# Two chained cross-attention and feed-forward layers: the maxima of block 0 and block 8 copied from ScalarE's queue, loads moved later, and the last feed-forward chunk in halves

## The chip, the cores and the metric
The kernel runs on one core of a Trainium2 chip. The metric is device time in microseconds (us). Engines: TensorE (PE, its weight loads PEld), VectorE (DVE), ScalarE (ACT), GpSimd (POOL), SyncE (SP, which here only issues DMAs). ScalarE issues DMAs as well, on a queue of its own. SBUF is the on-chip memory with 128 partitions, PSUM holds the eight accumulator banks of 128 x 512 f32.

## The reference
`x` is 4 x 1024 x 256, the context 4 x 77 x 256, all f32.
```
x = x + xattn0(layernorm(x), ctx, mask)   # 16 heads of 16, biases, softmax over 77 keys
x = x + experts(layernorm(x))             # 6 experts, the best 2 by a router, gelu
x = x + xattn1(layernorm(x), ctx)         # 16 query heads, one shared key and value head
x = x + ffn(layernorm(x))                 # 256 -> 1024 -> 256
  h = round256(h1 + b1);  y = piecewise-linear gelu(h) on 32 segments, round256
  out = round256(y @ w2 + b2)             # round256: to multiples of 1/256
```
Products are made to f32 accuracy: each operand is split into a high part (fp32r) and a low rest, and three products are added.

## The kernel before
The 4096 rows of x are eight blocks (G) of 512. Every engine has one program written out by hand in `build`; they meet only by semaphores (`wait_ge`, `then_inc`). There is no planner: what stands ahead in an engine's code runs first.

**Setup and the attention of block 0.** Keys, values and the first block's queries are made. A score of head i is one product of a stacked operand: `qst` holds per head pair, on partitions 0 to 95, high and low parts of the queries (`stack_queries`, L249, three DMAs of 256 KB for each half c of the heads, SBUF to SBUF), on partitions 96 and 97 the negated row maxima (`stack_maxima`, L260, one DMA of 32 KB in 16 rows of 2 KB) and on 98 to 127 part of the mask (`stack_low`, L242: 47 rows of 2 KB into `mm`, then 240 rows of 2 KB into `qst`). `l_kst` is the stacked key operand (twelve DMAs, L912). The maxima come from `max_unit` (PE), `take_maxima` (DVE), `turn_maxima` (PE) and `maxima` (ACT, writes `mt`). The first score of a block (`score`, i = 0, L400) waits for `mt_stacked`, `low_moved`, `stacked[0]`, and so for these DMAs; i = 8 waits for `stacked[1]`. `leading(G, c)` (ACT, L298) may overwrite `qh` only when the stacking DMAs of the block before have landed.

SP's code (L896 on) issues in this order for block 0: `stack_low`, six key copies, queries c = 0, six key copies, the maxima, queries c = 1, then mask 1 and two loads of 1 MB of x (L921). In the loop over G it then issues for block n = G + 1: `stack_low`, the queries of both halves, the mask of n + 1, the maxima of n. DMAs of one issuing engine go through one queue. In the loop, while block G is scored, block n's queries and maxima are made, the one after is normed, and block p = G - 1 is divided and projected.

**Values.** `vall` needs four batches b of two products of context and Wv and one of the bias (L1522); PE makes them after the maxima of block 0 were turned. ACT norms block 1 (L1138) and then copies the values (L1140).

**POOL in the setup** norms block 1 (`invert(1)`), then builds the masked keys of batches 1 to 3 (L1004, 16 operations), `wol`, then the mask parts of block 1.

**Layer 1** starts after the experts, as block G = 8 (`BLOCKS`): SP issues queries c = 0, the maxima, queries c = 1 (L959), and then the row loads `row0` (512 KB, the first row of w1 broadcast) and `rows` (L963). From G = 9 on the loop of L966 is used.

**The feed-forward** runs k = 0 to 63, eight chunks of 128 features for each block. Each chunk passes `hidden` (PE), `early` (DVE, writes `ffixed`), `gelus` (ACT, two), `climb` (POOL, `frise`), `interpolate` (DVE, `fpart`), `grow` (POOL) or `finish` (DVE, `fy`), `leading` (ACT, two: rounding in bank `YR`, then `fyh`), `rest` (DVE, `fyl`) and `output` (PE, 12 products). `YR` is one bank, so the leading of k waits for the rest of k - 1 (L744). At the end come `round_output` (ACT), `add` (DVE, two halves) and one store of 512 KB per block (L976).

## Time and profile before
| | |
|---|---|
| median of 3 runs | 789.33 us (789.02 to 789.87) |
| the profiled execution | 787.69 us, its span 785.5 us |
| busy share of the span | PE 93%, PEld 70%, DVE 82%, ACT 65%, POOL 47% |
| chain that ended last | PE 54%, DVE 19%, issue 8%, ACT 7%, DMA 7%, POOL 4% |
| DMA in the chain | qst<-mt 5% |
| mean granted TensorE clock | 0.991 of full |

The span runs from the first to the last instruction on the core; 2.2 us of the execution lie outside. "Issue" in the chain is time in which an engine waited for nothing that the profile attributes, so a wait for a DMA whose landing it could not pair may stand there. Times in the rows are us from the span's start.

### The profile page before, as it was taken

The page shows a single profiled execution, that of the slowest core. Times are in us where ns is not written, and L with a number is a line of the kernel's source. Part 1 is how long each engine was busy: PE and PEld are TensorE (multiplying, and loading weights), DVE is VectorE, ACT ScalarE, POOL GpSimd, SP SyncE. Part 2 cuts the span into 40 slices and gives each one's busy share as a digit, 9 for nine tenths or more (in the row PEclk, how much of TensorE's full clock was granted, in tenths as well). Part 3 has the DMA queues.
Part 4 walks back from the last instruction along what each step waited for, and adds up shares of the span by engine and source line. Part 5 has one row for each costly group of instructions (what it writes and reads, how often), then busy time and mean ns, then how long its engine had stood idle before and what let it go on. Part 6 is the DMA issues. An engine that isn't in the chain of part 4 may idle for free.

```text
span 785.5 us, 13554 instructions
## 1 busy us (share of the span) xinstructions
PE 729.2 (93%) x4372; PEld 549.3 (70%) x4372; DVE 644.6 (82%) x1546; ACT 514.0 (65%) x943; POOL 373.0 (47%) x323
## 2 busy tenths in 40 slices
PE   4799999999999999999997999999989999999995
PEld 3566666766558888888874555555568888888985
DVE  7648778777878878888897888998788999999995
ACT  3446556565654456555436777677778989989885
POOL 6374444334222223232214232232259999999884
PEclk9889999999999999999999999999999999999999
DMA  7975634654210000001029665755200000000001
GB/s 234 134 209 121 139 76 93 119 120 88 68 36 1 1 1 7 1 1 55 1 41 143 89 82 76 131 76 77 30 1 1 2 28 28 28 28 2 28 28 54
DMA packets 25101, 48.64 MB, mean 62 GB/s; under 512 B 3686, under 2 KB 7016, under 8 KB 24520
## 3 DMA queue, kind: packets, MB, share of 16 engines
q1 hardware_dynamic: 23366, 46.54, 30.6%
q10 hardware_dynamic: 1666, 1.24, 0.5%
q8 instruction: 36, 0.59, 0.3%
q14 instruction: 33, 0.27, 0.1%
HBM read 12.12 MB, written 4.19 MB: 21 GB/s over the span
## 4 chain that ended last, share of the span: by engine, by line
PE 54%; DVE 19%; issue 8%; ACT 7%; DMA 7%; POOL 4%; SPq 0%; ACTq 0%; DVEq 0%; POOLq 0%
PE bank L141 15%; PE bank L649 6%; PE bank L436 6%; PE bank L413 6%; DMA qst<-mt 5%; PE bank L424 5%; PE bank L388 5%; DVE mx L342 4%; PE bank L416 3%; DVE fpart L768 3%; PE bank L812 3%; PE bank L391 2%; DVE x L617 2%; DVE fyl L780 2%; DVE ffixed L762 2%
## 5 line engine op out<-in xcount | busy, mean ns | idle before, releaser
L316 ACT ACTIVATE pt<-bank 77x512 f32<-77x512 f32 x256 | 141.1, 589 | 78.2 <-PE bank L416 58.3
L342 DVE TENSOR_REDUCE mx<-bank 128x4 f32<-128x308 f32 x256 | 109.0, 471 | 22.5 <-PE bank L391 12.3
L413 PE MATMUL bank<-qst,l_kst 128*77 128x512 f32 (+1 forms) x256 | 102.8, 417 | 15.8 <-DMA qst<-mt 9.8
L721 POOL TENSOR_TENSOR frise<-fg,fg 128x512 f32<-128x512 f32 x64 | 101.3, 1583 | 6.7 <-ACT fg L739 1.5
L388 PE MATMUL bank<-l_kblk,qh 128*128 128x308 f32 x256 | 81.3, 336 | 10.1 <-DVE mx L342 5.7
L284 POOL TENSOR_TENSOR ol<-ot,oh 128x512 fp32r<-128x512 f32 x32 | 41.4, 1294 | 94.4 <-ACT oh L321 50.2
L617 DVE SCALAR_TENSOR_TENSOR x<-bank,eweight,x 128x256 f32<-128x256 f32 x192 | 79.6, 477 | 4.1 <-PE bank L649 3.8
L413 PEld LDWEIGHTS bank<-qst,l_kst 128*77 128x77 f32 (+1 forms) x256 | 36.5, 146 | 65.1 <-ACT pt L316 24.1
L103 POOL TENSOR_TENSOR rstd<-var,minus_half 128x4 f32<-128x4 f32 x32 | 34.4, 1076 | 100.1 <-DVE var L98 52.2
L114 ACT ACTIVATE xn<-x,shift,rstd 128x256 f32<-128x256 f32 (+1 forms) x128 | 67.2, 594 | 17.1 <-POOL shift L105 17.1
L388 PEld LDWEIGHTS bank<-l_kblk,qh 128*128 128x128 f32 x256 | 48.0, 192 | 42.8 <-issue 33.1
L812 PE MATMUL bank<-fw2h,fyh 128*128 128x256 f32 x256 | 73.4, 287 | 4.8 <-DVE fyl L780 4.6
L728 POOL TENSOR_TENSOR fy<-fpart,fg 128x512 f32<-128x512 f32 x48 | 68.5, 1428 | 9.8 <-DVE fpart L768 6.8
L812 PE MATMUL bank<-fw2l,fyh 128*128 128x256 f32 x256 | 72.0, 281 | 0.0
L812 PE MATMUL bank<-fw2h,fyl 128*128 128x256 f32 x256 | 71.8, 281 | 0.0
L424 PE MATMUL bank<-pt,l_vall 128*32 128x512 f32 x512 | 68.2, 604 | 1.3 <-DVE ut L347 0.9
L768 DVE SCALAR_TENSOR_TENSOR fpart<-ffixed,frise 128x512 f32<-128x512 uint16 x64 | 58.2, 911 | 11.2 <-POOL frise L721 11.2
L518 POOL TENSOR_TENSOR ehl<-eh,ehh 128x512 fp32r<-128x512 f32 x16 | 20.7, 1293 | 80.6 <-ACT ehh L534 80.6
L649 PE MATMUL bank<-ew2h,ehh 128*128 128x256 f32 x192 | 55.8, 291 | 2.9 <-DVE x L617 2.9
L532 ACT ACTIVATE eh<-bank 128x512 f32<-128x512 f32 x48 | 28.7, 598 | 41.5 <-PE bank L141 40.5
L812 PEld LDWEIGHTS bank<-fw2h,fyh 128*128 128x128 f32 x256 | 48.2, 188 | 10.8 <-DVE fyl L780 8.9
L649 PE MATMUL bank<-ew2l,ehh 128*128 128x256 f32 x192 | 54.1, 282 | 0.0
(176 smaller groups left out, 2117.0 us busy)
## 6 DMA issues: line engine op xcount, KB each, us to landing
qst<-qh SPq DMA_DIRECT2D x64, 256.0 KB, 6.5
qst<-ql SPq DMA_DIRECT2D x32, 256.0 KB, 8.8
out<-x SPq DMA_DIRECT2D x8, 512.0 KB, 2.6
qst<-ml SPq DMA_DIRECT2D x8, 480.0 KB
x<-in_x SPq DMA_DIRECT2D x3, 1024.0 KB, 12.4
weights<-in_mlp_w SPq DMA_DIRECT2D x2, 1024.0 KB, 5.0
mraw<-in_mask SPq DMA_DIRECT2D x8, 154.0 KB
x<-in_x SPq DMA_DIRECT2D x2, 512.0 KB, 5.8
```

The costliest lines, as they stand in the source:

```text
L141: last = self.nc.tensor.matmul(out, w, a, start=(first and k == 0), stop=(k == len(ops) - 1))
L316: self.nc.scalar.activation(self.pt[0:T, i // 4 % 2, i % 4, :], self.bank_of(G, i)[0:T, :], ACT.Exp).then_inc(self.probs, 1)
L342: self.nc.vector.reduce_max(out, banks[u % len(banks)][:, 0:4 * T].rearrange("q (p par t) -> q p par t", p=2, par=2), AX.X).then_inc(self. ...
L388: last = self.nc.tensor.matmul(bank, self.qh[:, c, tile], keys, start=True, stop=not layer.masked)
L413: last = self.nc.tensor.matmul(out, layer.kst[rows, layer.stack(c * HC + 2 * k + par), b * T:(b + 1) * T], self.qst[rows, self.slot(G), c ...
L424: last = self.nc.tensor.matmul(self.U[32 * k:32 * k + 32, :], layer.vall[:, self.batch(G), layer.value(c * HC + 2 * k + par), :], self.pt[ ...
L617: last = self.nc.vector.scalar_tensor_tensor(tile, part, self.weight[:, g % 2, 2 * k + t, e:e + 1], tile, ALU.mult, ALU.add)
L649: last = self.nc.tensor.matmul(self.OUT[k][:, t * D:(t + 1) * D], a[:, e % self.R, tile], w[:, e, :], start=(j == 0), stop=(j == 2))
L721: self.nc.gpsimd.tensor_tensor(self.rise[:, k % 2, :], self.g1[:, k % self.R, :], self.g0[:, k % self.R, :], ALU.subtract).then_inc(self.r ...
L728: self.nc.gpsimd.tensor_tensor(self.y[:, k % 2, :], self.part[:, k % 2, :], self.g0[:, k % self.R, :], ALU.add).then_inc(self.y_ready[0], 1)
L768: self.nc.vector.scalar_tensor_tensor(self.part[:, k % 2, :], self.fractions[:, k % self.R, :, 0], 2.0 ** -16, self.rise[:, k % 2, :], ALU ...
L812: last = nc.tensor.matmul(self.OUT[2 * (g % 2) + t // 2][:, t % 2 * D:(t % 2 + 1) * D], a[:, k % self.R, t * P:(t + 1) * P], w[:, c, :], s ...
```

## The change
**Maxima on ScalarE's queue.** `stack_maxima` of blocks 0 and 8 is issued by ACT right behind its `maxima`, no longer by SP. SP's queries c = 1 follow c = 0 without the maxima's wait in between.

**Loads.** Mask 1 goes ahead of the second six key copies. The two 1 MB loads of x are no longer issued in the setup but in the loops G = 0 and G = 1, behind the queries of block n and ahead of the mask and the maxima of block n. `row0` and `rows` go behind the queries of block 9.

**Setup order.** PE makes batch 0 of the values ahead of block 0's queries. ACT copies the first values ahead of norming block 1. POOL builds the masked keys before `invert(1)`, and makes mask parts 1 before `wol`. In G = 0 block 1's queries are made after scores 1 and 2 instead of 0 and 1, with the readers' order to match.

**The tail.** Chunk k = 63 is cut in two halves of 256 columns on all engines. Its climb and growth go from POOL to DVE. The last block's rounding waits per half, and its store is made as two of 256 KB.

```
@@ FeedForward: new
+    def climb_half(self, dve, h):
+        dve.wait_ge(self.tail["g"], h + 1)
+        dve.wait_ge(self.part_ready, BLOCKS * FC - 2)
+        self.nc.vector.tensor_tensor(self.half(self.rise, h), self.half(self.g1, h), self.half(self.g0, h), ...
+    def leading_half(self, act, h):
+        k = BLOCKS * FC - 1
+        bank = (self.YR[k], self.LN)[h][:, 0:N // 2]
+        act.wait_ge(self.tail["y"], h + 1)
+        act.wait_ge(self.yl_ready, k)
...
@@ SP, setup
-                    if c == 0:
-                        att.stack_queries(sp, 0, 0)
-                att.stack_maxima(sp, 0)
-                att.stack_queries(sp, 0, 1)
-                att.load_mask(sp, 1, d["mask"])
-                for b in range(2, B):
-                    tiles = slice(2 * b * NT, 2 * (b + 1) * NT)
-                    sp.dma_start(x[:, tiles, :], d["x"][:, tiles, :]).then_inc(xr_in, 16)
+                    att.stack_queries(sp, 0, c)
+                    if c == 0:
+                        att.load_mask(sp, 1, d["mask"])
@@ SP, loop over G
+                        if G < 2:
+                            tiles = slice(2 * (G + 2) * NT, 2 * (G + 3) * NT)
+                            sp.dma_start(x[:, tiles, :], d["x"][:, tiles, :]).then_inc(xr_in[G], 16)
                         if n + 1 < BLOCKS:
                             att.load_mask(sp, n + 1, d["mask"])
                         att.stack_maxima(sp, n)
@@ SP, layer 1
-                att.stack_queries(sp, BLOCKS, 0)
-                att.stack_maxima(sp, BLOCKS)
-                att.stack_queries(sp, BLOCKS, 1)
+                for c in range(C):
+                    att.stack_queries(sp, BLOCKS, c)
@@ ACT, setup and layer 1
                 att.maxima(act, 0, FIRST_MAX[0])
-                norm.norm(act, 1)
-                act.wait_ge(v_clear, 2)
+                att.stack_maxima(act, 0)
                 for k in range(2):
+                    if k == 1:
+                        norm.norm(act, 1)
...
                 att.maxima(act, BLOCKS, FIRST_MAX1[0])
+                att.stack_maxima(act, BLOCKS)
@@ SP, the stores
-                for g in range(BLOCKS):
+                for g in range(BLOCKS - 1):
...
+                for k in range(2):
+                    tiles = slice((BLOCKS - 1) * NT + 2 * k, (BLOCKS - 1) * NT + 2 * k + 2)
+                    sp.wait_ge(ff.added, 2 * (BLOCKS - 1) + k + 1)
+                    sp.dma_start(out[:, tiles, :], x[:, tiles, :]).then_inc(ff.stored, 16)
```

SP's queue from the end of the first key copies on, before (qst, qh, ql, mt as above, mraw the mask):
```order
L254 DMA qst<-qh 32x4x512 [waits qh_ready]
L254 DMA qst<-qh 32x4x512
L257 DMA qst<-ql 32x4x512 [waits ql_ready]
L912 DMA l_kst<-l_kh 16x4x308
...
L262 DMA qst<-mt 2x8x512 [waits mt_ready]
L254 DMA qst<-qh 32x4x512 [waits qh_ready]
L254 DMA qst<-qh 32x4x512
L257 DMA qst<-ql 32x4x512 [waits ql_ready]
L240 DMA mraw<-in_mask 77x512 [waits mask_ready]
L921 DMA x<-in_x 128x2048 x2
L245 DMA mm<-ml 47x512 [waits mask_ready]
L246 DMA qst<-ml 30x8x512
```
The same queue in the changed kernel, from block 1's mask on (first the last rows of block 0's queries):
```order
L257 DMA qst<-ql 32x4x512 [waits ql_ready]
L245 DMA mm<-ml 47x512 [waits mask_ready]
L246 DMA qst<-ml 30x8x512
L254 DMA qst<-qh 32x4x512 [waits qh_ready]
L254 DMA qst<-qh 32x4x512
L257 DMA qst<-ql 32x4x512 [waits ql_ready]
L254 DMA qst<-qh 32x4x512 [waits qh_ready]
L254 DMA qst<-qh 32x4x512
L257 DMA qst<-ql 32x4x512 [waits ql_ready]
L1000 DMA x<-in_x 128x2048
L240 DMA mraw<-in_mask 77x512 [waits mask_ready]
L262 DMA qst<-mt 2x8x512 [waits mt_ready]
```
Block 0's maxima have left the queue, and a load of x (L1000) has moved from ahead of block 1's stacking to right ahead of block 1's mask and maxima.

DVE at the end of the program, before:
```order
L768 SCALAR_TENSOR_TENSOR fpart<-ffixed,frise 128x512 [waits fy_ready0,frise_ready]
L780 SCALAR_TENSOR_TENSOR fyl<-bank,fyh 128x512 [waits fused,fyh_ready] x2
L789 SCALAR_TENSOR_TENSOR x<-bank,x 128x512 [waits fr_ready] x2
L780 SCALAR_TENSOR_TENSOR fyl<-bank,fyh 128x512 [waits fused,fyh_ready]
L789 SCALAR_TENSOR_TENSOR x<-bank,x 128x512 [waits fr_ready] x2
```
and in the changed kernel (L743 and L757 are the climb and the growth that POOL did):
```order
L743 TENSOR_TENSOR frise<-fg_154,fg_153 128x256 [waits fpart_ready,ftail_g] x2
L751 SCALAR_TENSOR_TENSOR fpart<-ffixed,frise 128x256 [waits fy_ready0,ftail_rise] x2
L855 SCALAR_TENSOR_TENSOR fyl<-bank,fyh 128x512 [waits fused,fyh_ready]
L757 TENSOR_TENSOR fy<-fpart,fg_153 128x256 [waits fyr_ready,ftail_part] x2
L864 SCALAR_TENSOR_TENSOR x<-bank,x 128x512 [waits fr_ready] x2
L855 SCALAR_TENSOR_TENSOR fyl<-bank,fyh 128x512 [waits fused,fyh_ready]
L774 SCALAR_TENSOR_TENSOR fyl<-bank,fyh 128x256 [waits fused,ftail_yh] x2
L864 SCALAR_TENSOR_TENSOR x<-bank,x 128x512 [waits fr_ready] x2
```
Two additions to x of block 6 (the first L864 row) now stand ahead of the rest of chunk 62 instead of behind it.

## Rows read from the trace of the kernel before
**Rows 1.** Chain that ended last, 15 to 66 us: start, length, what.
```profile
16.40 4.36 DVE l_kblk L1301 x16
...
29.23 0.86 PE bank L1525 x4
...
35.48 1.02 PE bank L127 x8
36.50 4.09 issue
40.59 0.68 PE bank L413
...
61.11 3.25 DMA qst<-mt
```
**Rows 2.** Timeline of SP's queue, setup: start, length of the issue, line.
```profile
23.23 0.61 SPq L257 DMA_DIRECT2D qst<-ql  x1
...
29.88 0.70 SPq L262 DMA_DIRECT2D qst<-mt  x1
...
31.91 0.60 SPq L257 DMA_DIRECT2D qst<-ql  x1
...
46.44 0.70 SPq L245 DMA_DIRECT2D mm<-ml  x1
```
**Rows 3.** Timeline of POOL, masked keys of batches 1 to 3.
```profile
32.09 10.34 POOL L1004 TENSOR_TENSOR l_kblk<-l_kh,hsel 128x231 fp32r<-128x231 f32 x16
```
**Rows 4.** Tile qst, DMAs issued from 21.5 to 24 us.
```profile
DMA to landing us min/median/max: 5.8/7.3/11.2
```
**Rows 5.** Tile qst, DMAs issued from 30 to 33 us.
```profile
DMA to landing us min/median/max: 7.2/8.8/11.4
```
**Rows 6.** Stretches: length, busy of each engine, PEclk, DMA share, GB/s.
```profile
36.00:40.00 4.00, 0.50 (x5) 0.26 (x3) 3.19 (x13) 1.70 (x4) 3.53 (x7) 0.76 1.04 136
...
41.00:44.00 3.00, 3.00 (x8) 2.25 (x7) 0.00 (x0) 0.59 (x1) 2.56 (x5) 0.50 1.00 362
...
56.00:58.00 2.00, 1.72 (x12) 1.12 (x15) 1.36 (x5) 1.97 (x5) 0.37 (x1) 1.00 1.07 198
...
62.30:63.40 1.10, 1.10 (x10) 0.16 (x8) 0.53 (x1) 1.10 (x4) 0.00 (x0) 1.00 0.11 39
```
**Rows 7.** DMA queues from 8 to 13 us: q1 is SP's, q10 ACT's.
```profile
q1 hardware_dynamic: 299, 1.56, 81.9%
q10 hardware_dynamic: 387, 0.34, 21.6%
```
**Rows 8.** Chain that ended last, 411.5 to 422 us (layer 1's start).
```profile
412.20 0.68 SPq L262
...
414.24 6.85 DMA qst<-ql
```
**Rows 9.** Waits from 412 to 436 us: total, times, longest.
```profile
PE bank L388 <- ACT qh L305: 2.1, 1, 2.1
```
**Rows 10.** Stretches around layer 1's start.
```profile
409.50:413.50 4.00, 2.85 (x23) 2.33 (x22) 3.65 (x10) 1.07 (x2) 0.00 (x0) 1.00 0.00 0
...
415.00:416.90 1.90, 1.30 (x6) 1.12 (x7) 1.90 (x6) 1.46 (x2) 0.74 (x3) 1.00 1.05 129
```
**Rows 11.** Chain that ended last, 772 to 786 us.
```profile
775.99 0.70 DVE fyl L780
...
776.77 0.61 ACT bank L745
...
778.79 1.70 PE bank L812 x12
...
781.13 0.69 DVE x L789
```
**Rows 12.** Tile x from 775 to 786 us.
```profile
DMA to landing us min/median/max: 2.6/2.6/2.6
```
**Rows 13.** Costliest groups of the page: busy, mean ns of one, idle before.
```profile
L617 DVE SCALAR_TENSOR_TENSOR x<-bank,eweight,x 128x256 f32<-128x256 f32 x192 | 79.6, 477 | 4.1 <-PE bank L649 3.8
```

More of the change, by code:

```diff
@@ new lines, in gelus_half @@
+    def gelus_half(self, act, h):
+        k = BLOCKS * FC - 1
+        act.wait_ge(self.tail["fixed"], h + 1)
+        self.wait_y(act, k - self.R)
+        index = self.halves[:, k % self.R, h * (N // 2):(h + 1) * (N // 2), 1]
+        self.nc.scalar.activation(self.half(self.g0, h), index, ACT.Gelu, scale=SEGMENT)
+        self.nc.scalar.activation(self.half(self.g1, h), index, ACT.Gelu, bias=self.segment[:, 0:1],
+                                  scale=SEGMENT).then_inc(self.tail["g"], 1)
@@ new lines, in rest_half, with output_half @@
+    def rest_half(self, dve, h):
+        k = BLOCKS * FC - 1
+        dve.wait_ge(self.tail["yh"], h + 1)
+        dve.wait_ge(self.used, k - self.R + 1)
+        self.nc.vector.scalar_tensor_tensor(self.half(self.yl, h), (self.YR[k], self.LN)[h][:, 0:N // 2], TO_256TH,
+                                            self.half(self.yh, h).bitcast(F32), ALU.subtract,
+                                            ALU.subtract).then_inc(self.tail["yl"], 1)
+    def output_half(self, pe, h):
+        k = BLOCKS * FC - 1
+        g, c = divmod(k, FC)
+        pe.wait_ge(self.tail["yl"], h + 1)
+        for t in (2 * h, 2 * h + 1):
+            for a, w in ((self.yh, self.w2h), (self.yh, self.w2l), (self.yl, self.w2h)):
+                last = self.nc.tensor.matmul(self.OUT[2 * (g % 2) + h][:, t % 2 * D:(t % 2 + 1) * D],
+                                             a[:, k % self.R, t * P:(t + 1) * P], w[:, c, :], start=False,
+                                             stop=(t % 2 == 1 and a is self.yl))
+        last.then_inc(self.tail["used"], 1)
@@ L1007, in _ @@
                     pool.wait_ge(kblk_more, head + 1)
+                norm.invert(pool, 1)
+                att.mask_parts(pool, 1)
                 pool.wait_ge(woh_ready, 1)
@@ L1260, in _ @@
                         ff.leading(act, 0)
-                    if k > 0:
+                    if k == BLOCKS * FC - 1:
+                        for h in range(2):
+                            ff.gelus_half(act, h)
+                    elif k > 0:
                         ff.gelus(act, k)
@@ L1320, in _ @@
                     if n < BLOCKS:
-                        for c in range(C):
-                            att.rest(dve, n, c)
+                        att.rest(dve, n, 0)
+                        if G > 0:
+                            att.rest(dve, n, 1)
                         att.take_maxima(dve, n, range(0, 2), att.X)
+                        if G == 0:
+                            att.rest(dve, n, 1)
                     if p >= 0:
@@ L1464, in _ @@
                         ff.rest(dve, 0)
-                    if k >= 2:
+                    if k == BLOCKS * FC - 1:
+                        for h in range(2):
+                            ff.early_half(dve, h)
+                    elif k >= 2:
                         ff.early(dve, k)
@@ L1511, in _, with values @@
                     norm.turn(pe, 0, c, att.W[c])
+                def values(b):
+                    bank = att.SC[b // 2][0:T, D * (b % 2):D * (b % 2) + D]
+                    for k in range(C):
+                        nc.tensor.matmul(bank, ctx[:, k, b * T:(b + 1) * T], wv0[:, k, :], start=(k == 0), stop=False)
+                    last = nc.tensor.matmul(bank, ones_row[:, :], rows[:], start=False, stop=True)
+                    if b % 2:
+                        last.then_inc(v_done, 1)
+                pe.wait_ge(vo_in, 64)
+                pe.wait_ge(cleared, 1)
+                values(0)
                 pe.wait_ge(wql_ready, 1)
@@ L1519, in _ @@
                 att.turn_maxima(pe, 0, FIRST_MAX[0])
-                pe.wait_ge(vo_in, 64)
-                pe.wait_ge(cleared, 1)
-                for b in range(B):
-                    bank = att.SC[b // 2][0:T, D * (b % 2):D * (b % 2) + D]
-                    for k in range(C):
-                        nc.tensor.matmul(bank, ctx[:, k, b * T:(b + 1) * T], wv0[:, k, :], start=(k == 0), stop=False)
-                    last = nc.tensor.matmul(bank, ones_row[:, :], rows[:], start=False, stop=True)
-                    if b % 2:
-                        last.then_inc(v_done, 1)
+                for b in range(1, B):
+                    values(b)
                 for c in range(C):
```

100 lines of the change are left out of this document (72 added, 28 removed).

## Prediction
> **What bounds the kernel now.** I read the table of busy shares first: PE works 93% of the span, so a gain must come from stretches in which PE stands still, runs at its lower clock, or has ended. The profile's chain by kind has DMA at 7%, 5% of it `qst<-mt`, the copy of the maxima. The chain of waits then shows three such places, which are the three that the change touches.
>
> At the start (from 15 us) the chain goes through the masked keys, the values and the transposes of the maxima, which end at 36.50; then 4.09 us of "issue" follow, and the first score stands at 40.59 [rows 1]. SP's queue explains it: the maxima are issued at 29.88, behind key copies and queries c = 0 issued at 23.23 [rows 2], which land after up to 11.2 us [rows 4], at 23.23 + 11.2 = 34.4. The DMA share in 36 to 40 is 1.04 [rows 6]: `mt` waits behind rows, not for a product. After the pause the granted clock is 0.50, that is 1.2 GHz of 2.4, in 41 to 44 (0.76 in 36 to 40, with the pause in it). The second place is the hand-over to block 1: its maxima land at 61.11 + 3.25 = 64.4, and only then G = 1 begins [rows 1]. The third is layer 1's start, where the chain ends on `ql` landing at 421.1 [rows 8]. The tail from 776 on is a plain chain of rounding, rest, products, rounding, add and store [rows 11, 12].
>
> The profiled execution took 787.69 us, span 785.5; the median is 789.33, so 1.64 is added at the end. A change under 0.2% (1.6 us) can't be told from none here.
>
> **Start, block 0.** Before: `mt` is first in, first out behind SP's rows. After: ACT issues it at about 29.9 (the wait for `maxima` is the same). Two queues on one engine take turns: from 8 to 13 us SP's and ACT's queue passed 299 and 387 packets [rows 7], near one for one. One row of `mt` is 2 KB; at 136 GB/s over 16 engines [rows 6] it takes 2048 B / 8.5 GB/s = 0.24 us. Alone, `mt` lands in 3.25 [rows 1], so at 33.1; with 8 rows of SP's between its own 8 (8 x 0.24 = 1.9) at 35.0. Queries c = 0, which would have landed at 34.4, get its 8 rows: 36.3. The first score stands at the later one, 36.4; the bounds are 33.1, if nothing is in the way but `mt` (then PE's own end of the transposes at 35.7 decides), and 38.9, if all 16 rows count double at 0.24 each on top of 35.0.
>
> The Trainium skill (DMA: Bandwidth & Descriptors, "Queues, rings and completion order") says that an engine changes between rings at packets of typically 9 to 17 descriptors; by it `mt` would wait for a group of up to 17 rows, an estimated 17 x 0.24 = 4.1 us, and the first score would be at about 37.2 to 39. The counts of rows 7, near one for one, speak for small turns.
>
> Other work that must be done before 36.4: the four batches of values take 35.48 - 29.23 = 6.25, or 1.56 a batch [rows 1]. One batch is moved ahead, into the time in which PE waits for the masked keys, which last until 16.40 + 4.36 = 20.8 [rows 1]: hidden there; if it is not, the queries come up to 0.6 late. The masked keys of POOL, 10.34 us [rows 3], come ahead of `invert(1)`, ending near 31 instead of 42.4; the inverse of block 1 ends at the same time. I price this at nothing: block 1's norm is wanted after the first scores. Gain at the first score: 40.6 - 36.4 = 4.2.
>
> **Block 1, where most of it is lost.** Before, 64.4 - 40.6 = 23.8 us lie between the first scores of block 0 and block 1 [rows 1]. I take 1.0 of it as PE's wait at the end (in 62.3 to 63.4 the DMA share is 0.11 and only the maxima's path is missing [rows 6]) and 2.0 as the price of the lower clock (about 4 us at 0.50 [rows 6]). Were PE alone the bound, G = 1 would start at 36.4 + 21.0 = 57.4. But the rows must be through as well. Queries c = 1 of block 0 were issued at 31.91 and landed after 11.4 [rows 2, 5], at 43.3. They lose nothing by the change, but `mt` no longer ahead is matched by mask 1 ahead (0.8) and the interleaved rows (0.8): some 44.9. Then comes block 1's stack: 94 KB of `mm`, 480 KB of low parts and 1536 KB of queries, 2.11 MB. At 198 GB/s [rows 6] that is 10.7 us. Before, this stack began when the 2 MB of x were through (48.4: 43.3, 0.8 of mask, and 4.3 at rates between 362 [rows 6] and its half) and ended at 63.4 with the long last queue: 15.0. The first figure leaves out that a few engines carry more than the others (share 0.11 [rows 6]); the second has waits for products in it. I take 13.5, nearer the second: 58.4. The load of x (1 MB at 362 GB/s [rows 6]: 2.9) now stands ahead of block 1's maxima: 61.3. Mask, `mt` and the release add 1.0: G = 1 starts at about 62.2 instead of 64.4, gain 2.2. PE then pauses 62.2 - 57.4 = 4.8, longer than today's 1.0, and as after the pause at 36.5 the clock probably falls: I take 1.0 of the 2.0 back (0 to 2.0). Start in sum: **-1.2**, bounds -6 (no backlog, below) and +2.5 (slow backlog, below). The second load of x goes in G = 1, where no long backlog is left; 2.9 us of it ahead of block 2's maxima are covered by a block of about 24 us.
>
> The Trainium skill (same page, "Why a DMA increments its semaphore by 16 and not by 1") says that a DMA is spread over the largest k up to 16 that divides both slowest dims, so 47 rows of `mm` go to one engine and `mt`'s 2 partitions to two. The trace agrees: share 0.11 in 62.3 to 63.4 is about two of 16 engines. By it one engine carries 47 rows more than the others, an estimated 47 x 0.17 = 8 us at the 198 GB/s above, and the stack would take more than the 13.5: the sum goes by the two figures above.
>
> **Layer 1.** SP now issues queries c = 1 right behind c = 0, into 409.5 to 413.5, where the DMA share is 0.00 [rows 10], rather than behind the maxima issued at 412.20 [rows 8]. Their 6.85 us of landing [rows 8] begin some 6 us earlier, so PE's one wait of 2.1 for `qh` of ACT, which waited for that landing [rows 9, 8], goes. What is late next: `mt`, issued by ACT at 412.2, meets those rows: eight at 2048 B / (129 / 16 GB/s) = 0.25, of which some four lie ahead: +1.0 on the first score of G = 8. The longer pause of PE ahead of it can cost clock: I take 0.7 (0 to 2). `row0` (512 KB, 1.4 us at 362 GB/s [rows 6]) and `rows` now go behind block 9's queries and ahead of its maxima, so the maxima's landing for G = 9 is hidden by less: of the 2.1 about nothing beyond 2.1 can be kept. Sum: -2.1 + 1.0 + 0.7 = **-0.4**, bounds -2.1 and +1.9 (nothing gained of the wait, and all that `row0` takes and the clock added).
>
> **Tail.** Chunk 63's climb and growth leave POOL for DVE in halves; halves on ACT cost between 0.30 and 0.61 (the whole [rows 11]), on DVE 0.35 to 0.48 (128x256 in another group [rows 13]). Two additions of block 6 stand ahead of the rest of 62 on DVE (2 x 0.69 [rows 11]), so `fyl` of 62 is done near 777.3 instead of 776.7. PE then has 1.4 for 62 and 1.7 for 63 [rows 11], and ends at 780.6 against 778.79 + 1.70 = 780.5: nothing. After that only the second half's rounding (0.6) and one add (0.69) follow, 1.3 against rounding and two adds today, 1.9: -0.6. The last store has half the size: of 2.6 [rows 12] I take 0.5 off (0 to 0.9). **-1.1**, bounds -1.7 and +0.4 (if the additions ahead of 62's rest delay it by all of 1.4, with no store gain).
>
> **Sum.** -1.2 - 0.4 - 1.1 = -2.7; 787.69 - 2.7 + 1.64 = **786.6**. The forecast's own range is 784.5 to 788.3.
>
> **Rivals.** (1) The backlog doesn't bind block 1: its stack takes the 10.7 of the 198 GB/s and its maxima get through, so G = 1 starts at 57.4 to 58.5: -6 at the start, -0.9 in layer 1, -1.1 in the tail, **781.3**. For it: today's 15.0 has waits in it. Against: share 1.00 or more in every stretch of block 0 that I looked at [rows 6]. Chance 0.15. (2) Slower: the load of x ahead of block 1's maxima. If the stack passes at the 129 to 136 GB/s of rows 6 and 10 instead of 198, 2.11 MB take 16 us: 44.9 + 16 = 60.9, x and mask at that slower sharing 4, release 1: G = 1 at 66, +1.6, and clock +1.4; with +0.5 in layer 1 and -1.0 in the tail +2.5, **791.8**. It decides from the point where `mt` of block 1 lands later than about 65.4. For it: only one of those stretches shows a high rate with SBUF to SBUF rows. Against: block 1's rows ran faster than block 0's (198 against 136). Chance 0.20. (3) The moved copy was hidden: G = 1 starts where it did, since SP's queue is just as full; the earlier first score only makes PE wait later. Start 0, layer 1 +0.3, tail -1.1: **788.5**. For it: the DMA share in rows 6 is full. Against: 1 MB less ahead of block 1's stack. Chance 0.20. The forecast has 0.45.
>
> **Chances.** Faster by over 0.2% (below 787.75): the forecast with 0.36 of its 0.45, rival 1 with 0.15, and 0.05 of rival 3: 0.56. Within: 0.09 and 0.13 of rival 3 and 0.01 of rival 2: 0.23. Slower: 0.21, most of it rival 2. The range of 782.5 to 790.5 takes in the forecast, rival 3 and the nearer parts of the two others.
>
> **What would show it.** First score at about 36.4 (39 would say that `mt` waits for groups of rows; below 36, that the bound is PE). First product of G = 1 at 62, with a pause of 5 us ahead of it and a clock of 0.5 after it; a start at 58 is rival 1, at 64.4 rival 3, at 66 rival 2. In layer 1, first score at 416.6 less the shift, and no 2.1 of `qh` in the waits. In the tail, one rounding and one add behind the last product, and a landing near 2.1. It would be wrong altogether if a wait appeared that is in none of these places.

## The result: slower by 0.6%

| | before | changed |
|---|---|---|
| median | 789.33 us (788.84 to 789.90, 5 runs) | 793.43 us (792.90 to 794.58, 5 runs) |
| ratio | | 1.0059, 95% interval 1.0044 to 1.0073 |
| profiled execution, span | 787.69, 785.5 us | 793.25, 791.3 us |
| mean granted clock | 0.991 | 0.983 |

The forecast was 786.6 in a range of 782.5 to 790.5: wrong in sign and size. (The ratio is not the quotient of the two medians, which is 1.0052.) The two profiled spans differ by 5.8 us. I follow that difference at five marks, the last column being what is added between one mark and the next.

| mark (us) | before | changed | later by | added |
|---|---|---|---|---|
| first score of block 0 | 40.59 | 42.80 | 2.2 | 2.2 |
| first score of block 1 | 64.40 | 67.95 | 3.55 | 1.3 |
| block 8's maxima issued | 412.20 | 416.56 | 4.4 | 0.8 |
| block 10's maxima issued | 453.16 | 459.93 | 6.8 | 2.4 |
| end of the span | 785.5 | 791.3 | 5.8 | -1.0 |

### The profile page after: what moved, and what is told of

It reads as the page before. It is cut to its first block, busy times and chain, and to the rows that moved or that the text cites. A ratio compares the mean times of both kernels' runs of the same rounds, so it can differ in the third digit from the quotient of the medians.

```text
span 791.3 us, 13574 instructions
## 1 busy us (share of the span) xinstructions
PE 733.5 (93%) x4372; PEld 551.6 (70%) x4372; DVE 649.2 (82%) x1553; ACT 514.4 (65%) x947; POOL 369.4 (47%) x321
## 4 chain that ended last, share of the span: by engine, by line
PE 52%; DVE 18%; issue 9%; DMA 7%; ACT 7%; POOL 5%; SPq 1%; ACTq 0%; DVEq 0%; POOLq 0%
PE bank L141 15%; PE bank L649 7%; PE bank L436 6%; PE bank L413 6%; DMA qst<-mt 5%; PE bank L424 5%; PE bank L388 4%; DVE mx L342 3%; PE bank L416 3%; DVE fpart L843 3%; PE bank L887 2%; DVE ffixed L837 2%; PE bank L391 2%; DVE x L617 2%; DVE fyl L855 2%
## 5 line engine op out<-in xcount | busy, mean ns | idle before, releaser
L801 POOL TENSOR_TENSOR fy<-fpart,fg 128x512 f32<-128x512 f32 x47 | 66.8, 1421 | 9.7 <-DVE fpart L843 6.8
L532 ACT ACTIVATE eh<-bank 128x512 f32<-128x512 f32 x48 | 28.7, 597 | 41.6 <-PE bank L141 40.5
```

## The profile after

The chain of waits of the changed kernel at the start, in the columns of [rows 1]:
```profile
42.80 0.68 PE bank L413
...
64.86 3.04 DMA qst<-mt
67.95 0.46 PE bank L413
```
ACT's timeline (start, length, operation), and under it SP's queue:
```profile
28.93 0.59 ACT L310 ACTIVATE mt<-bank 16x512 fp32r<-16x512 f32 x1 [4.58 <-PE bank L397]
29.55 0.76 ACTq L262 DMA_DIRECT2D qst<-mt  x1
```
```profile
23.87 0.55 SPq L240 DMA_DIRECT2D mraw<-in_mask  x1
...
28.27 1.56 SPq L254 DMA_DIRECT2D qst<-qh  x2
29.88 0.60 SPq L257 DMA_DIRECT2D qst<-ql  x1
...
54.34 0.60 SPq L1000 DMA_DIRECT2D x<-in_x  x1
...
64.86 0.71 SPq L262 DMA_DIRECT2D qst<-mt  x1
```
The maxima are issued at 29.55, as early as forecast, and the score that waits for them still starts at 42.80. They do not get ahead of the rows that SP issued before them. What is new is what lies ahead of them: mask 1 (23.87), and the first rows of queries c = 1 (28.27), which stood behind them before (30.64, between two rows of [rows 2]). Block 1's start again hangs on its own maxima, which land in about the same time (3.04, [rows 1] has 3.25) but are issued 3.75 us later.

The same stretches as in [rows 6] and those around layer 1's start:
```profile
36.00:40.00 4.00, 0.89 (x5) 0.49 (x3) 3.07 (x11) 1.71 (x3) 2.60 (x3) 0.50 0.96 127
...
44.00:48.00 4.00, 4.00 (x11) 2.82 (x10) 0.00 (x0) 1.19 (x2) 3.76 (x4) 0.50 0.22 55
...
412.00:416.00 4.00, 3.40 (x14) 2.08 (x14) 3.99 (x12) 0.06 (x1) 0.00 (x0) 0.66 1.06 125
416.00:420.00 4.00, 3.51 (x16) 3.11 (x16) 2.57 (x7) 1.58 (x3) 0.31 (x1) 0.50 0.85 100
```
Three of the same stretches in the kernel before:
```profile
44.00:48.00 4.00, 4.00 (x18) 3.01 (x17) 1.51 (x3) 2.46 (x4) 3.77 (x4) 0.89 0.44 176
...
412.00:416.00 4.00, 2.33 (x18) 2.09 (x18) 3.65 (x10) 2.54 (x4) 1.15 (x3) 1.00 0.52 97
416.00:420.00 4.00, 3.77 (x18) 2.78 (x16) 3.08 (x13) 1.67 (x3) 1.21 (x2) 1.00 1.08 133
```
PE is at 1.2 GHz (granted clock 0.50) in all of 44 to 48 and in 416 to 420, where it was at or near 2.4 GHz before (0.89 and 1.00). In 44 to 48 it makes 11 products in 4.00 busy us instead of 18: a late first score is followed by slow products, and the pause is paid for twice.

The chain of waits in layer 1, from block 9's maxima on, changed kernel, then before:
```profile
436.73 4.15 DMA qst<-mt
440.93 1.14 PE bank L413 x2
442.07 3.72 PE bank L141 x12
```
```profile
435.60 0.68 PE bank L413 x2
436.28 2.74 PE bank L141 x12
...
453.16 2.89 DMA qst<-mt
```
The copy of block 9's maxima takes 4.15 us, with the row loads ahead of it; in the kernel before it took 2.92 (432.64 to 435.55 in its chain). The 14 products behind it take 1.14 + 3.72 = 4.86 us instead of 3.42. The wait of 2.1 us of [rows 9] is gone, as forecast; its place is taken by a later first score of block 8 (4.0 us from the start of ACT's copy to the score before, 411.59 to 415.60; 5.8 now, 415.94 to 421.75).

The end, in the columns of [rows 11]:
```profile
784.41 1.68 PE bank L887 x12
786.09 0.72 PE bank L784 x6
...
786.89 0.59 ACT bank L829
...
787.50 1.33 DVE x L864 x2
```
PE ends at about 787.5; 3.8 us are left to the end of the span, against 785.5 - 780.5 = 5.0 before [rows 11].

## The experiments

Ratios are of each kernel to the kernel before on the same chip (788.4 to 788.8 us there, 789.33 for the first row), in brackets the 95% interval. They are not quotients of the medians, which can differ by 0.15% (keys late: 1.0021), so a cost taken from ratios and one taken from medians can be 1 us apart. Scores 0 and 1 come from one profiled execution each. "Score 0" and "score 1" are the first scores of blocks 0 and 1 (40.6 and 64.4 in the kernel before).

| kernel | median | ratio | score 0 | score 1 |
|---|---|---|---|---|
| changed | 793.43 | 1.0059 [1.0044, 1.0073] | 42.8 | 67.95 |
| tail alone | 786.79 | 0.9978 [0.9967, 0.9988] | 40.75 | 64.96 |
| tail, engines' order | 788.10 | 0.9991 [0.9979, 1.0003] | 40.78 | 65.95 |
| changed, layer 1 back | 791.14 | 1.0035 [1.0022, 1.0048] | 43.41 | 68.03 |
| layer 1 alone | 792.80 | 1.0047 [1.0033, 1.0061] | 40.86 | 65.88 |
| the same, row loads early | 791.31 | 1.0033 [1.0022, 1.0045] | 40.48 | 64.83 |
| changed, maxima on SP | 793.44 | 1.0057 [1.0042, 1.0072] | 42.40 | 67.75 |
| changed, SP waits too | 796.10 | 1.0096 [1.0083, 1.0109] | 43.79 | 69.02 |
| changed, mask 1 back | 794.13 | 1.0061 [1.0041, 1.0080] | 42.45 | 67.76 |
| changed, mm split | 793.36 | 1.0054 [1.0040, 1.0068] | 42.84 | 68.14 |
| tail, maxima on ACT | 790.91 | 1.0029 [1.0018, 1.0040] | 41.90 | 65.39 |
| tail, x late | 792.86 | 1.0046 [1.0033, 1.0058] | 40.74 | 67.66 |
| tail, keys late | 790.06 | 1.0006 [0.9990, 1.0022] | 36.48 | 65.11 |
| tail, mm split | 790.83 | 1.0025 [1.0015, 1.0034] | 35.98 | 65.80 |
| maxima and mask first | 789.76 | 1.0015 [1.0002, 1.0029] | 36.15 | 65.55 |
| the same, x late | 789.64 | 1.0004 [0.9992, 1.0017] | 35.83 | 64.66 |
| the same, maxima on ACT | 790.85 | 1.0023 [1.0012, 1.0034] | 36.09 | 66.12 |
| maxima and mask first, mm split | 786.66 | 0.9969 [0.9955, 0.9983] | 36.28 | 63.05 |
| the same, block 1's maxima first | 786.44 | 0.9971 [0.9957, 0.9985] | 36.21 | 60.35 |

### One part at a time

**The tail alone** (only the halves of chunk 63 and the store in two parts):

> Kernel before with only the change at the end: chunk 63 in halves, its climb and growth on DVE, the last store in two parts. Theory: from the end of PE's last product to the end of the span it takes 3.8 us instead of 5.0 (as in the changed kernel: 791.3 - 787.5 against 785.5 - 780.5), and the last product itself ends where it did, within 0.4 us: -1.0 +- 0.4 us, ratio 0.9987. Rival: the additions of block 6 ahead of the rest of chunk 62 push PE's last products back by 1 us or more and the gain behind them is used up: 0 +- 0.3.

Measured 0.9978: 1.7 us won, a little more than expected. In its profile the last product ends at 781.3 and the span at 785.1, so the 3.8 us came as forecast; where the rest of the gain lies isn't shown. **Layer 1 alone**, with the edit

```
-                att.stack_queries(sp, BLOCKS, 0)
-                att.stack_maxima(sp, BLOCKS)
-                att.stack_queries(sp, BLOCKS, 1)
+                for c in range(C):
+                    att.stack_queries(sp, BLOCKS, c)
...
+                att.stack_maxima(act, BLOCKS)
```
and the row loads behind block 9's queries:

> Kernel before with only layer 1's change: block 8's maxima on ACT's queue, queries c = 1 issued right behind c = 0, row loads behind block 9's queries. Theory A (a copy on ACT's queue does not overtake rows that SP has issued earlier): the maxima land some 9 to 9.5 us after issue less the rows that passed before it, 5 to 6 us after issue instead of 3.4, the first score of block 8 comes about 2 us late, and the lower clock may come on top: +2 to +3.5 us. Rival B (layer 1 is innocent, what looks like its loss is carried there from the setup): -0.5 +- 0.5 us.

Measured 1.0047, 3.7 us (4.2 by the medians): A, and above its upper end. With the row loads where they were:

> Kernel before with block 8's queries c = 1 issued behind c = 0 and its maxima on ACT's queue, but the row loads where they were. Against the run with all of layer 1's change (792.8) and the kernel before (788.6). Theory F (the row loads ahead of block 9's maxima cost 1.2 us of landing and 1.4 us of lower clock behind the longer pause): 2.0 to 3.0 us under 792.8, and the landing of block 9's maxima takes 2.9 us again instead of 4.2. Rival G (the cost is all at block 8's maxima, which wait for the queries' rows): within 0.8 us of 792.8.

Measured 1.0033, so 2.6 us are the cost of block 8's maxima and some 1.1 us that of the row loads; the intervals of the two kernels overlap, so the second figure isn't clear of none. The landing is: block 9's maxima take 2.93 us here and 4.11 with the row loads ahead. Both theories named a part; F's 2.0 to 3.0 us were too high. PE's first scores of block 8 in this kernel:
```profile
418.99 1.10 PE L413 MATMUL bank<-qst,l_kst 98*77 98x512 f32 x2 [4.43 <-issue]
```
ACT's copy begins at 412.22: 6.8 us to the score instead of 4.0. **Setup without SP's part, and layer 1 undone:**

> Kernel before with the new tail and the setup's new order on PE, ACT, POOL and DVE (one batch of values ahead of the queries, values copied before block 1 is normed, masked keys ahead of the inverse, block 1's queries behind scores 1 and 2), but SP's queue, the maxima and layer 1 as before. Theory: nothing of it is on the path, within 0.6 us of the kernel with the new tail alone (786.8). Rival: queries of block 1 made one score later cost PE 1 to 2 us of waits in block 0, 788 to 789.

> Changed kernel with layer 1 wholly as before; the setup and the tail are the changed kernel's. Theory (the parts add): the changed kernel's 793.4 less layer 1's cost, which was 4.2 us beside the kernel before with that part alone and 2.9 us by the stretch from block 7's to block 10's maxima: 789.3 to 790.5; what is left above the kernel with the new tail alone (786.8), 2.5 to 3.5 us, is the setup's. Rival (the setup costs nothing, layer 1 all): 786.8 +- 0.7.

Measured 788.10 and 791.14. The new order on PE, ACT, POOL and DVE costs 1.0 us (0.9978 to 0.9991; the intervals overlap, but block 1 also starts 1.0 us later, at 65.95), which is its rival and not its theory, SP's new order with the maxima's new queue 3.5 us more (0.9991 to 1.0035), layer 1 another 1.9 us (1.0035 to 1.0059), where it cost 3.7 alone. The theory that the parts add gave 789.3 to 790.5 for the second kernel, a little too low. Each step is uncertain by about 1.5 us, and the parts need not add, since each moves the stretches of lower clock.

### Queue or order of issue

Four edits of the changed kernel's queue: the maxima back on SP ahead of queries c = 1 (in block 8 too); SP held until the maxima are made; mask 1 back; later, the split of `mm`.

```
+                    if c == 1:
+                        att.stack_maxima(sp, 0)      # first kernel: in place of ACT's
+                        sp.wait_ge(att.mt_ready, 1)  # second kernel: instead of the line above
                     att.stack_queries(sp, 0, c)
...
```

> Changed kernel with only this undone: the maxima of blocks 0 and 8 are issued by SP again, ahead of queries c = 1. Theory A (order of issue decides, the queue doesn't): the maxima of block 0 land by 41.5 us instead of 42.7 (mask 1 is still ahead of them) and those of block 8 3.5 us after issue instead of 5.2; the time falls from 793.4 by 1.5 to 4 us, to 789.5 to 792. Rival B (the setup's other moves on POOL, PE and ACT and the load of x cost the time): the landing comes earlier but the time stays within 0.8 us of 793.4.

> Changed kernel with one addition: SP waits for the maxima to be made before it issues queries c = 1, in the setup and in layer 1; the maxima stay on ACT's queue. So SP's rows that are issued before the maxima are those of the kernel before plus mask 1. Theory A (rows issued earlier on the other queue go first): block 0's maxima land at 40 to 41.5 us, as on SP's queue, and the time is that of the kernel with the maxima back on SP, within 0.8 us. Rival C (ACT's queue takes turns with SP's row by row from its issue on, and it was only the queries c = 1 that got in between): they land at 35 to 37 us, and the time is 2 us or more under the one with the maxima on SP.

> Changed kernel with only mask 1 moved back: its load is issued behind block 0's queries c = 1 instead of ahead of the second six key copies. Theory D (the 77 rows of the mask lie on 11 of the 16 engines, 7 rows of 0.26 us each = 1.8 us, ahead of the maxima): block 0's maxima land 1.8 us earlier, at 40.9 instead of 42.7, and the time falls by 1.0 to 2.5 us from 793.4. Rival E (rows of queries c = 1 ahead of the maxima are what costs): they land at 42.2 or later and the time falls by less than 0.5 us.

None of them is faster: 1.0057, 1.0096 and 1.0061. With the maxima on SP, mask 1 still lies ahead (score 0 at 42.40); with mask 1 back, queries c = 1 do (42.45); with both it is 42.8 to 43.4, with neither 40.6. So either alone costs about 1.8 us of the first score, the second adds less, and D's gain of 1.8 us for the mask did not come. Nor did A's 1.5 to 4 us: with the maxima on SP block 8's first score does come 2.7 us earlier (419.05), but a wait of 2.2 us for `qh` is back and the clock is at 0.50 from 430 to 436.

Why the two don't add is seen in the landings. In the traces each copy of the maxima has two, one for each of the DMA engines that carry its 16 rows, and the score needs both:

| kernel | first landing | second |
|---|---|---|
| before | 35.7 | 40.3 |
| tail alone | 36.0 | 40.45 |
| tail, maxima on ACT (below) | 37.9 | 41.6 |
| changed, maxima on SP (mask 1 ahead) | 38.3 | 42.1 |
| changed, mask 1 back (queries c = 1 ahead) | 41.85 | 42.1 |
| changed | 41.6 | 42.5 |
| changed, mm split | 42.5 | 42.5 |
| tail, mm split | 34.1 | 34.2 |
| tail, keys late | 33.3 | 33.3 |

In the kernel before, half of the maxima was there at 35.7 and only one engine was late. Mask 1 delays both halves by about 2 us; queries c = 1 delay the early half by 6 us, up to the late one, and the late one by 1.7 us.

A is wrong on the queue: the kernel with the maxima on SP and the one in which SP waits have the same order of issue, and the one with the maxima on ACT has its first score 1.4 us later and takes 2.7 us more. The cleaner test of the queue leaves the order of issue as it was before:

```
-                att.stack_maxima(sp, 0)
+                sp.wait_ge(att.mt_ready, 1)       # the maxima are issued by ACT
                 att.stack_queries(sp, 0, 1)
```

> Kernel with the new tail alone, and the maxima of blocks 0 and 8 issued by ACT; SP waits until they are made and then issues queries c = 1, so the order of issue is that of the kernel before and only the queue differs. Theory A (rows that SP issued earlier go first): block 0's maxima land at 40 to 42 us, 10 us or more after their issue, block 8's 3.4 to 4.5 us after, and the time is 0 to 1.5 us above 786.8. The prediction's step (the two queues take turns row by row from the issue on): they land at 35 to 36.5 us, 5 to 6 us after issue.

PE's first scores of blocks 0 and 8 in it, then those of the kernel with the tail alone, and ACT's issue for block 8:
```profile
41.90 0.68 PE L413 MATMUL bank<-qst,l_kst 128*77 128x512 f32 x1 [5.05 <-issue]
...
419.38 1.11 PE L413 MATMUL bank<-qst,l_kst 98*77 98x512 f32 x2 [4.12 <-issue]
```
```profile
40.75 0.68 PE L413 MATMUL bank<-qst,l_kst 128*77 128x512 f32 x1 [4.13 <-issue]
...
416.79 0.67 PE L413 MATMUL bank<-qst,l_kst 98*77 98x512 f32 x2 [0.93 <-issue]
```
```profile
412.93 0.59 ACT L310 ACTIVATE mt<-bank 16x512 fp32r<-16x512 f32 x1 [4.62 <-PE bank L397]
413.54 0.65 ACTq L262 DMA_DIRECT2D qst<-mt  x1
```
This is the experiment that decides the step. On a queue of its own, issued 0.2 us later and behind the same rows, the maxima of block 0 land no earlier but 1.1 us later (first score 41.90 against 40.75). The edit also lets SP issue queries c = 1 in the same instant instead of 0.7 us behind the maxima, so what is shown is that the second queue does not get ahead, and not what it costs with nothing beside it. For block 8, where nothing lies ahead, it is 6.45 us from copy to score (412.93 to 419.38) against 4.0 (412.75 to 416.79 in the tail's own run): queries c = 1, issued by SP at 413.54 too, now go ahead of the maxima instead of behind them. The first rows of the maxima start at 415.84, 2.3 us after issue, when SP's first copy of queries c = 1 ends (415.77 to 416.12).

ACT's queue in this kernel in two stretches, 34.5 to 36.6 and 415.8 to 417.8 us (packets, MB, share of 16 engines):
```profile
q10 hardware_dynamic: 9, 0.02, 6.3%
...
q10 hardware_dynamic: 16, 0.03, 13.1%
```
6.3% of 16 engines is one engine's whole time and 13.1% that of two. So once they start, the eight rows of an engine follow each other, one every 0.25 us, with no time left for rows of SP's between them. The prediction's sum mixed them one for one; here they wait for what SP issued before, and then go as one group.

The kernel takes 4.1 us more than the tail alone in the median (786.79 to 790.91). A forecast the landing of block 0 (40 to 42) and missed the rest: block 8's maxima land 5.6 us after issue instead of 3.4 to 4.5, and the price was to be at most 1.5 us. Of the 4.1 us almost nothing comes from block 0: ACT's copy for block 8 begins only 0.2 us later (412.93 against 412.75). The loss is made behind it, by a first score 2.6 us later and a clock at 0.50 from 418.1 to 424.9. Also with the maxima first, where ACT's queue was tried once more:

> The first kernel of these with one difference: the maxima are issued by ACT, and SP waits for them to be made before it issues mask 1. Issue times and order are the same, only the queue differs. Theory A (what was issued earlier goes first, the queue is indifferent): landing of the maxima within 0.7 us and the time within 0.8 us of the kernel beside it. Rival K (a second queue costs: its rows stand behind all that SP issues soon after): the landing takes 5 us or more instead of 3.5, and the first score is 1.5 us or more later.

790.85 against 789.76, score 1 at 66.12 against 65.55: the same sign, near what can be told. The maxima land at 34.8 instead of 33.1, between theory and rival; score 0 doesn't show it (36.09 against 36.15), because PE's own transposes last until then.

### What block 1's start waits for

Three edits that each bring the maxima of block 0 forward or take rows away, all on top of the tail:

> Kernel before with the new tail, and SP's setup in another order: block 0's maxima are issued ahead of the second six key copies instead of behind them. Theory (order on SP's queue sets the first score; block 1 starts 24 us behind it, by PE's own work and not by a backlog of rows): the maxima land at 36 to 37.5 us instead of 40.5, the first score at 36.4 to 37.8, block 1 starts 3 to 4 us earlier than in the kernel before, and the time is 3 to 4 us under the kernel with the new tail alone (786.8): 783 to 784. Rival (the backlog of x and block 1's stack binds next, as the prediction had it): block 1 starts at 62 or later and at most 1.5 us are gained.

> Kernel with the new tail alone, and the loads of x moved into the loops G = 0 and G = 1 as in the changed kernel. Theory (in the kernel before block 1's start is set by PE's work and by the rows about equally, and x is not on either way): block 1's maxima land at 64 to 66 us and the time is within 0.8 us of 786.8. Rival (the load ahead of block 1's maxima delays them): they take 5 us or more to land instead of 3.2, and the time is 1.5 us or more above 786.8.

> Kernel with the new tail alone, and each block's copy of 47 rows into mm issued as two, of 32 and of 15 rows. Now the 47 rows are on one DMA engine; split, an engine has 2 or 3. Theory L (block 0's first score and block 1's start wait for the queue of that one engine): at 0.26 us a row the setup's 44 rows less are not all on the path, but block 0's maxima land 1 to 4 us earlier and block 1's 0.5 to 2 us earlier; the time falls by 0.5 to 2.5 us from 786.8. Rival M (all sixteen engines are full until then, one more or less does not matter): within 0.5 us, or 0.3 us above it for the additional issues.

```
-        sp.dma_start(self.mm[T:SPLIT, ...], self.ml[LOW:T, :]...).then_inc(self.low_moved, 16)
+        for a, b in ((LOW, LOW + 32), (LOW + 32, T)):
+            sp.dma_start(self.mm[T + a - LOW:T + b - LOW, ...], self.ml[a:b, :]...).then_inc(self.low_moved, 16)
```

Keys late, PE's timeline: its wait for mask 1 and the one ahead of block 1.
```profile
46.05 0.53 PE L391 MATMUL bank<-id,mh 128*128 128x308 f32 x1 [3.69 <-POOL mh L270]
...
65.11 0.46 PE L413 MATMUL bank<-qst,l_kst 128*77 128x512 f32 x1 [1.08 <-DMA qst<-mt]
```
x late, chain of waits:
```profile
60.70 6.92 DMA qst<-mt
...
67.66 0.65 PE bank L413
```
and the same score in PE's timeline:
```profile
67.66 0.65 PE L413 MATMUL bank<-qst,l_kst 128*77 128x512 f32 x1 [4.41 <-DMA qst<-mt]
```
`mm` split:
```profile
44.62 0.63 PE L392 MATMUL bank<-id,mh 128*128 128x308 f32 x1 [2.78 <-POOL mh L271]
...
65.80 0.71 PE L414 MATMUL bank<-qst,l_kst 128*77 128x512 f32 x1 [3.35 <-DMA qst<-mt]
```
With the keys late or `mm` split, block 0's maxima land at 33.3 and 34.2 us instead of 40.45, by far the largest step made here, and both kernels are slower than the tail alone (790.06 and 790.83 against 786.79): PE then waits for `mh`, the high part of mask 1, whose load still lies at the queue's end, and block 1 starts at 65.1 and 65.8. With `mm` split the clock is at 0.50 from 64.8 to 71.6, behind that pause, and block 8's first score is 4.2 us later than in the tail's run (420.96). (With the keys late both halves land at 33.3 though `mm` is whole, so the 47 rows delay the maxima only together with the key copies.) The forecasts of 783 to 784 and of a gain of 0.5 to 2.5 us were both wrong. With x late, the load ahead of block 1's maxima makes their landing take 6.92 us instead of 3.25 [rows 1], and 4.4 us of pause stand ahead of block 1; the time rises by 6.1 us in the median, 5.4 by the ratios, more than the pause, with the clock at 0.50 from 67.8 to 71.2. That is the prediction's rival 2, mechanism and place, in a kernel where nothing else hides it.

With the maxima and mask 1 both ahead of the second key copies, and the engines in their new order:

> Kernel before with the new tail, the new order of the setup on PE, ACT, POOL and DVE, and SP's queue in the order queries c = 0, maxima, mask 1, second six key copies, queries c = 1, loads of x; layer 1 as before. In the run with the key copies behind the maxima, block 0's maxima landed at 33.6 us, but PE then stood until 46.05 us for mask 1, which lay at the end of the queue. Theory H (both are needed: the maxima and mask 1 ahead of the other rows): maxima at 33.6, mask parts made by POOL from about 36 on, no wait of PE above 1 us between 37 and 57 us, block 1's maxima land at 60 to 62 us instead of 64.6, and the time is 3 to 4.5 us under the kernel with the new tail alone: 782.5 to 784. Rival (the backlog of x and block 1's queries binds next): they land at 64 us or later and the time is within 1 us of 786.8.

> The same with the two loads of x in the loops G = 0 and G = 1 as in the changed kernel. Theory I (2 MB of x ahead of block 1's stack are 4.3 us of the queue, and matter only where that stack is late): if block 1's queries are late in the kernel beside it, this one is up to 2 us faster; if not, both are within 0.6 us. Rival J: the load ahead of block 1's maxima makes their landing take 5 us or more instead of 3.2, and it is 1 to 2 us slower.

> The kernel with the maxima and mask 1 first in SP's queue (789.8, its block 1 maxima issued at 56.8 and landed at 65.4), with the same split of mm. There most engines had landed block 1's queries by 61.0, the last one at 64.5. Theory L: the maxima of block 1 land at 60 to 62.5 us, PE's pause ahead of them shrinks from 6.2 to 2 or 3 us, and the time falls by 2.5 to 4.5 us, to 785.5 to 787.3. Rival M: they land at 64 us or later, within 1 us of 789.8.

PE's pause ahead of block 1, without and with the split, and last with block 1's own maxima ahead of its queries c = 1:
```profile
65.55 0.71 PE L413 MATMUL bank<-qst,l_kst 128*77 128x512 f32 x1 [6.23 <-DMA qst<-mt]
```
```profile
63.05 0.46 PE L414 MATMUL bank<-qst,l_kst 128*77 128x512 f32 x1 [2.97 <-DMA qst<-mt]
```
```profile
60.35 0.45 PE L414 MATMUL bank<-qst,l_kst 128*77 128x512 f32 x1 [0.71 <-DMA qst<-mt]
```
Without the split H fails: PE's work of block 0 ends at 59.3 instead of 65.5 (engines' order) and the rows do not come earlier. Block 1's maxima, issued at 56.77, land at 62.6 and 65.5, and in the pause the clock falls:
```profile
56.00:61.00 5.00, 3.33 (x23) 1.67 (x21) 4.17 (x9) 3.27 (x7) 0.00 (x0) 1.00 0.83 136
62.00:66.00 4.00, 0.45 (x1) 0.34 (x2) 0.09 (x2) 0.00 (x0) 1.01 (x1) 0.50 0.07 23
```
The DMA share in 62 to 66 is 0.07, about one engine of sixteen: L is right about which one. With the 47 rows spread, block 1 starts 2.5 us earlier, and this kernel beats the kernel before (0.9969 [0.9955, 0.9983]). It does not beat the tail that it contains by more than the noise (0.9978 [0.9967, 0.9988]), so its new setup is worth 0.7 us at best. Moving x there is neutral in the median (789.64 against 789.76) and brings block 1 0.9 us forward: inside I's "up to 2 us faster", and without J's loss.

> The fastest kernel so far (maxima and mask 1 first, mm split: 786.7) with block 1's queries c = 1 issued behind its maxima instead of ahead of them, and block 2's queries made behind scores 1 and 2 like block 1's. Theory (in that kernel block 1's maxima were issued at 57.5 us and landed at 63.2, behind its own queries' rows): they land 3 to 4 us after issue, at 60.5 to 61.5, and the time falls by 1 to 3 us, to 783.7 to 785.7. Rival (what is taken from block 1's start comes back as a wait for the late queries c = 1 at block 2's, or as a lower clock): within 1 us of 786.7, or above it.

Block 1 now starts at 60.35, 4.05 us before the kernel before, and the time stays (786.44 against 786.66): its rival. From the issue of block 1's maxima to that of block 7's it takes 148.5 us here and 146.1 before. That the late queries c = 1 come back as waits in block 1 fits this; it isn't shown row by row.

> Changed kernel with only the copy of 47 rows into mm issued as two, of 32 and 15 rows. Theory L (the one full DMA engine queue is what makes block 0's maxima late): they land 4 us or more earlier than the 42.7 us of the changed kernel, and block 1's start, which waited for PE's work behind the first score, comes 2 us or more earlier than 68.1; the time falls by 1 to 4 us from 793.4. Rival (all engines are as full; the maxima on ACT's queue wait for the queries c = 1 anyway): landing at 40.5 us or later and within 0.8 us of 793.4.

In the changed kernel the split does nothing (793.36, score 0 at 42.84), so there it is not that engine's queue: both halves of the maxima land at 42.5, behind the queries c = 1.

## Why the prediction was wrong, step by step

**Start, block 0: the step that failed.** "Two queues on one engine take turns ... near one for one", hence a first score at 36.4. It came at 42.80. The counts of [rows 7] are those of two queues fed together over 5 us; they say nothing of rows that one queue was given earlier, and nothing of the length of a turn, as equal groups give equal counts too. With the queue changed and the order kept the maxima land 1.1 us later, not 4 earlier, and their rows are not mixed one for one with SP's. That is shown. How an engine picks between queues is not: the first rows of the maxima start at 38.59 in the changed kernel, 9 us after issue, and at 34.53 where only the queue differs, and how many rows were ahead on the engine can't be read from the traces. The prediction named "39 would say that mt waits for groups of rows"; even that reading and its 37.2 to 39 were too early. The 36.4 itself could be reached: where the maxima land at 33 to 34, score 0 stands at 35.8 to 36.5, right behind PE's transposes, which the prediction let end at 35.7.

**Rows now ahead of the maxima.** I priced mask 1 at 0.8 us, for the wrong step (queries c = 1), and saw that queries c = 1 were no longer held back, but took this as a help to them and none of it as a cost to the maxima. Either alone is worth 1.8 us at the first score, both together 2.2 to 2.8.

**Block 1.** The prediction took 2.2 us off 64.4; it became 67.95. PE's work from score 0 to block 1's start took 25.15 us instead of 23.8: the clock at 0.50 until 48.1 instead of 44.9, and waits for block 1's later queries. The engines' new order, priced at nothing, costs about 1.0, again with overlapping intervals. The backlog of rows, on the other hand, is real: it was predicted at 62, and where score 0 was brought forward it held block 1 to 65 (maxima first), by one engine's queue and not by all rows together. In the changed kernel itself it doesn't bind, as the first score is late.

**The load of x** was priced inside that backlog, and the rival for it at 0.20. By itself it costs 5.4 to 6.1 us. In the changed kernel it hides behind the late first score (3.04 us to land); had the rest of the change worked, it would probably have been the next wait. Rival 2's 791.8 lies nearest to the 793.43, but by luck: its cause is absent here.

**Layer 1** was forecast at -0.4 with bounds of -2.1 and +1.9. It costs 3.7 alone and 1.9 on top of the rest. The wait of 2.1 is gone; in its place are a landing longer by 1.8 to 2.8 (forecast 1.0), `row0` ahead of block 9's maxima (1.2 us of landing), and the lower clock behind both pauses. The term of 1.0 took the maxima to pass after some four rows on each engine; they waited for a whole copy of SP's (till 415.84, issued at 413.54, in the run where only the queue differs), which is nearer to the groups that the prediction set aside. The bound of +1.9 was too tight because it added each once and the clock only in part.

**Tail.** Forecast -1.1. Between the last product and the end 1.2 us are saved; alone the tail brings 1.7. The step was right in size. Its form was not wholly: the two last additions still follow each other, as the first half's products wait behind chunk 62's (786.09), so both halves' adds stand behind the last product, and what is saved lies in the halved store (2.0 to 2.1 us to land instead of 2.6) and in the first rounding, which starts ahead of PE's end (786.89 against 787.5).

**Sum.** In place of -1.2 - 0.4 - 1.1 the profiled runs show +3.55 at the start, +0.8 between, +2.4 in layer 1 and -1.0 behind it. What stays open: the 0.8 us between block 1 and layer 1, and why the clock falls at 413 in the changed kernel, where PE worked 3.40 of 4.00 us, and not in the one before, where it worked 2.33. The fall isn't the change's own: with the tail alone the clock is at 0.50 from 411.8 to 415.2 too, in a kernel that is faster than the one before.

## What to carry to other kernels

Do not count on a transfer on another engine's queue to overtake what is already issued; in no run here did it. If a copy is urgent, keep bulk copies from being issued ahead of it, and that is what the wait in the old order did. Before a wait is moved forward, list all that the next stage needs (here the mask, the last rows of one engine's queue, the next maxima) and bring them forward together: of seven kernels with a first score at 36 instead of 40.6 us, only the two that brought mask 1 forward and emptied the one full DMA engine queue beat the kernel before, and these not the tail that did about as well alone (786.66 and 786.44 against 786.79). A pause made longer costs twice when the clock falls behind it, so a step that only moves a wait later can make a kernel slower.

## What the runs showed of the hardware

- The copy of 47 rows into `mm` loads one DMA engine far more than the others: splitting it in 32 and 15 brought the landing of the maxima, issued behind it, from 40.45 to 34.2 us, and without the split a share of 0.07, one engine of sixteen, is left in the last 4 us ahead of block 1.
- The copy of 32 KB takes 6.45 us from ACT's copy that makes it to its first use on ACT's queue and 4.0 on SP's, with 768 KB issued by SP in the same instant in the first case and right behind it in the second.
- On ACT's queue the eight rows of an engine go in one stretch of 2 us (one engine's whole time from 34.5 to 36.6 us, two engines' from 415.8 to 417.8), and start 4.3 and 2.3 us after issue.
- One kernel's time goes with its mean granted clock: keys late took 786.9 to 787.2 us at 0.992 to 0.995 and 789.6 to 791.1 at 0.985 to 0.989. Its profiled execution is one of the first (787.21); taken alone it would have told a gain that the median (790.06) doesn't show.
